# Attention block, one core: the last head group's PV in two sessions, with the row maxima's product behind it

## The chip, the cores and the metric

The kernel runs on one core of a Trainium2 chip. The metric is device time in microseconds (us) of one execution; lower is better. Every number is float32 in memory; the large products run as float32 or as float32 split in a high and a low part.

## What is computed

```python
def reference(x, w_qkv, b_qkv, w_proj, b_proj, pos_independent, ffn_kernel, input_scale, kernel_scale, ffn_bias):
    # x: 16 x 512 x 256; 16 heads of 16
    xn = _layernorm(x, axis=-1)
    qkv = xn @ w_qkv.T + b_qkv
    q, k, v = ...                                   # reshape to heads
    att = einsum('bhqd,bhkd->bhqk', q, k) / sqrt(16)
    att = att + bias                                # per head, from positions alone
    att = softmax(where(causal, att, -inf))
    attn = einsum('bhqk,bhkd->bhqd', att, v) @ w_proj.T + b_proj
    ffn = quantise_e4m3(xn.bf16) @ quantise_e4m3(ffn_kernel) + ffn_bias
    return x + attn + ffn
```

## The kernel before, in words

A **body** `b` handles one of the 16 batches and overlaps it with its neighbours. Bodies 0, 14 and 15 are written out; bodies 1 to 13 are a loop on every engine. A body has four **units** `g` of four heads each, and a unit has twelve **slots** `k`. I write a place as (unit, slot), so (0, 3) is slot 3 of the body's first unit.

In every slot TensorE (PE) makes two interleaved streams. `scores_T` (L640, L643) makes transposed scores of this unit into one of three banks `scoreT_a/b/c`; ScalarE (ACT) turns each into `probs` with an exponential (L925), GpSimd (POOL) masks the diagonal (L1201), and `pv` (L666) multiplies the masked probabilities of the *previous* unit with V and a column of ones. `scores` (L617) makes plain scores two units ahead into `score_a/b/c`, from which VectorE (DVE) takes row maxima (L1003). A slot's `scores_T` waits for the exponential of three slots earlier, its `scores` for the row maximum of three slots earlier. All waits are in order on an engine: what stands behind a waiting instruction waits too.

Other work hangs behind slots by tables of (unit, slot): `PV_AT` (PV of the previous unit; for unit 3 of body b-1 that is in body b), `MT_AT` (the product that transposes the maxima, L601), `QK_AT`, `V_AT`, `FF_AT` (the quantised product, L593), `PJ_AT`, `T_AT` (transpose of x two bodies ahead, L558). All of these write two banks in turn, `misc_a` and `misc_b`, and each waits until the former user of its bank was read. A PV stands whole in one place, except that of unit 0, which `PV_REST_AT` cuts: key tile 0 at (1, 0), tiles 1 to 3 at (1, 3).

The stations around the change:

- **Maxima to scores.** ACT `max_hi` (L840) in slot 2, PE `job_MT` (L601), ACT `max_T` (L844), then SP `load_max` issues four 4 KB transfers (L341). Slot 0 of the next unit waits for all four.
- **PV to the denominators.** ACT `out_T` (L898) copies PV's bank; then `send_attn` issues two transfers, `attn` (L354) and `denominators` (L355). For units 0 to 2 SP issues them (`regroup`); for unit 3 ACT itself does, right behind `out_T`, after a wait for that copy. DVE `invert` (L1010) takes reciprocals at (0, 6); SP stores them (`store_recips`, L396) and loads them spread over the rows of `xn` (`spread_recips`, L408); POOL divides (L1235) in unit 1.
- **x two bodies ahead.** PE transposes at (3, 9) into `misc_a` and `misc_b`; ACT copies each twice (`XH_evac` L821, `XB_evac` L824); DVE makes the low halves (`T_lo`, L985), of `misc_a` at (3, 10) and of `misc_b` at (0, 0). DVE's statistics of x stand in unit 1 (L973, L981).
- **FF.** Its second half writes `misc_b` at (2, 0), which QK's last low part (DVE L991, at (1, 10)) must have read.

## Time and profile before

| what | us |
|---|---|
| median of 3 runs | 810.89 |
| lowest, highest | 809.94, 812.63 |
| the profiled execution, whole time | 810.14 |
| its span in the profile | 808.4 |
| PE busy, of the span | 752.4 (93%) |
| DVE, ACT, POOL busy | 624.6, 578.6, 531.1 |

The span is the time between the first and last instruction of the profiled execution; 1.7 us of that execution lie outside it. A view of the profile is a timeline (instructions of one engine in order of time, in brackets the idle time before it and who ended it), a table of waits (who waited for whom, summed), or busy time by stretch. The loop repeats every 46.3 us; the rows below are from the body that starts at about 421.9 us, unless said otherwise.

### The profile page before, as it was taken

Reading aid. Unit: us, or ns where it says so; the run is one execution under the profiler, and the core shown is the slowest. Engines: PE = TensorE matmul, PEld = TensorE weight load, DVE = VectorE, ACT = ScalarE, POOL = GpSimd, SP = SyncE. Lnnn points to the kernel's source line nnn. Section 1 sums busy time; section 2 is a strip of 40 time slices with the busy share of each in tenths; the row PEclk is TensorE's granted clock in tenths of the full one; section 3 lists DMA queues with packets and bytes.
Section 4 is the critical chain, followed back from the end, with each engine's and each line's share of the span. In section 5 each row is a group of like instructions: output and inputs, shape, how many; then the busy total and the mean of one; then the engine's idle time right before and its main releaser. Section 6 shows DMA issues by size and latency. Waiting matters only on the chain.

```text
span 808.4 us, 23158 instructions
## 1 busy us (share of the span) xinstructions
PE 752.4 (93%) x6313; PEld 515.3 (64%) x6313; DVE 624.6 (77%) x2395; ACT 578.6 (72%) x1258; POOL 531.1 (66%) x525
## 2 busy tenths in 40 slices
PE   6889999999999999999999999999999999999883
PEld 3556566676666766666676667667676666667552
DVE  3869878887978888787887888798788878888612
ACT  3347868777877868777886777777787777777570
POOL 6435568676666767577666857666676767757570
PEclk8859999999999999999999999999999999999997
DMA  5603333534333253333434243443335334343202
GB/s 172 235 2 140 120 123 114 172 115 151 138 145 136 106 189 119 129 137 145 166 117 149 112 159 112 164 140 145 121 119 179 131 122 138 146 146 114 78 18 86
DMA packets 55612, 106.07 MB, mean 131 GB/s; under 512 B 10528, under 2 KB 30496, under 8 KB 55584
## 3 DMA queue, kind: packets, MB, share of 16 engines
q1 hardware_dynamic: 52680, 102.96, 36.2%
q10 hardware_dynamic: 2904, 2.77, 1.1%
q8 instruction: 13, 0.21, 0.1%
q14 instruction: 15, 0.12, 0.1%
HBM read 18.68 MB, written 8.91 MB: 34 GB/s over the span
## 4 chain that ended last, share of the span: by engine, by line
PE 69%; ACT 7%; DVE 7%; issue 6%; DMA 6%; SPq 3%; ACTq 1%; DVEq 1%; POOL 0%; POOLq 0%
PE misc_a L666 13%; PE misc_a L550 10%; PE misc_b L550 10%; PE scoreT_b L640 8%; PE scoreT_a L640 5%; PE score_a L617 4%; PE score_c L617 4%; DMA x_ring<-in_L_attn_x 4%; PE misc_b L666 3%; SPq L341 3%; ACT probs L925 3%; PE misc_b L601 2%; ACT xnT_hi L821 2%; PE scoreT_c L640 2%; DVE row_max L1003 1%
## 5 line engine op out<-in xcount | busy, mean ns | idle before, releaser
L1201 POOL TENSOR_SCALAR_AFFINE_SELECT probs<-probs 128x512 f32<-128x512 f32 x256 | 161.7, 642 | 231.1 <-ACT probs L925 229.5
L1003 DVE CUSTOM_DVE_ANT_0 score_b<-score_b,causal_mask_q 128x384 f32<-128x384 f32 (+3 forms) x321 | 162.0, 522 | 95.8 <-PE score_b L617 95.6
L1003 DVE CUSTOM_DVE_ANT_0 score_a<-score_a,causal_mask_q 128x512 f32<-128x512 f32 x319 | 174.9, 565 | 6.5 <-PE score_a L617 3.2
L925 ACT ACTIVATE probs<-scoreT_b 128x384 f32<-128x384 f32 (+1 forms) x256 | 134.4, 525 | 63.5 <-PE scoreT_b L640 21.1
L1003 DVE CUSTOM_DVE_ANT_0 score_c<-score_c,causal_mask_q 128x256 f32<-128x256 f32 (+3 forms) x384 | 172.0, 476 | 3.0 <-PE score_c L617 2.8
L925 ACT ACTIVATE probs<-scoreT_a 128x512 f32<-128x512 f32 (+1 forms) x256 | 145.4, 568 | 4.5 <-PE scoreT_a L643 3.7
L1003 DVE DVE_READ_ACCUMULATOR2_ANT row_max<- 128x1 f32 x1024 | 145.6, 142 | 0.0
L925 ACT ACTIVATE probs<-scoreT_c 128x384 f32<-128x384 f32 (+1 forms) x256 | 135.9, 531 | 3.4 <-PE scoreT_c L643 3.0
L666 PE MATMUL misc_a<-probs,v_ones 128*32 128x128 f32 (+3 forms) x1536 | 132.1, 440 | 0.4 <-POOL probs L1201 0.4
L640 PE MATMUL scoreT_b<-stacks 64*128 64x384 f32 (+3 forms) x320 | 120.0, 394 | 5.7 <-ACT probs L925 5.7
L617 PE MATMUL score_b<-stacks 64*128 64x384 f32 (+3 forms) x321 | 118.4, 401 | 1.4 <-DVE row_max L1003 1.4
L640 PE MATMUL scoreT_c<-stacks 64*128 64x256 f32 (+3 forms) x384 | 106.6, 309 | 8.9 <-ACT probs L925 8.9
L617 PE MATMUL score_a<-stacks 64*128 64x512 f32 x319 | 111.1, 380 | 2.7 <-DVE row_max L1003 2.6
L640 PE MATMUL scoreT_a<-stacks 64*128 64x512 f32 (+3 forms) x320 | 108.1, 358 | 5.0 <-DMA low_features<-neg_max_T 2.4
L640 PEld LDWEIGHTS scoreT_b<-stacks 64*128 64x128 f32 x320 | 57.0, 185 | 72.6 <-ACT probs L925 39.9
L617 PE MATMUL score_c<-stacks 64*128 64x256 f32 (+3 forms) x384 | 99.6, 313 | 0.5 <-DVE row_max L1003 0.2
L640 PEld LDWEIGHTS scoreT_c<-stacks 64*128 64x128 f32 x384 | 68.9, 187 | 15.9 <-ACT probs L925 14.0
L666 PEld LDWEIGHTS misc_a<-probs,v_ones 128*32 128x32 f32 x1536 | 59.7, 109 | 28.6 <-issue 12.3
L617 PEld LDWEIGHTS score_c<-stacks 64*128 64x128 f32 x384 | 65.8, 189 | 5.5 <-DVE row_max L1003 5.0
L617 PEld LDWEIGHTS score_a<-stacks 64*128 64x128 f32 x319 | 55.4, 188 | 20.4 <-DVE row_max L1003 16.9
L640 PEld LDWEIGHTS scoreT_a<-stacks 64*128 64x128 f32 x320 | 57.4, 187 | 12.0 <-issue 6.8
L898 ACT ACTIVATE out_T<-misc_a 128x512 f32<-128x512 f32 x48 | 28.7, 599 | 42.4 <-PE misc_a L666 42.4
(241 smaller groups left out, 1957.3 us busy)
## 6 DMA issues: line engine op xcount, KB each, us to landing
stacks<-qk_parts SPq DMA_DIRECT2D x128, 512.0 KB, 3.9
x_ring<-in_L_attn_x SPq DMA_DIRECT2D x16, 512.0 KB, 3.3
xn<-recips SPq DMA_DIRECT2D x31, 256.0 KB
out<-x_ring SPq DMA_DIRECT2D x15, 512.0 KB, 3.0
attn<-out_T SPq DMA_DIRECT2D x48, 128.0 KB, 2.6
stacks<-neg_max_T SPq DMA_DIRECT2D x128, 4.0 KB
attn<-out_T ACTq DMA_DIRECT2D x16, 128.0 KB, 2.7
low_features<-neg_max_T SPq DMA_DIRECT2D x124, 4.0 KB
```

Of the source, the lines that this page charges most:

```text
L341: eng.dma_start(max_rows(g, h), MTS[2 * TT * h:2 * TT * h + 2 * TT, g % 2, :].bitcast(F32)) \
L550: last = mm(o, l(ct), r(ct), start=(ct == 0 and i == 0), stop=(ct == CT - 1 and i == 2))
L601: last = mm(bank[0:HU * 2 * TT, 0:P], MX[:, g % 2, 32 * part:32 * part + 32], ident[:, :], start=(part == 0), stop=(part == 1))
L617: last = mm(SB_[n % 3][:, o:o + w], STK[rows, u, 0, P * qt:P * qt + P], STK[rows, u, 1, 0:w], start=True, stop=True)
L640: last = mm(bank, STK[rows, u, 1, P * j:P * j + P], STK[rows, u, 0, P * j:T], start=True, stop=(g >= 2))
L666: last = mm(bank[32 * i:32 * i + 32, P * j:T], VA[:, j, HU * g + i, :, :].rearrange("p d a -> p (d a)"), probs(g, j)[:, i, :], start=(j == ...
L821: A(XH[:, ct, :], misc_of("T", ct)[:, :], ACT.Copy).then_inc(xh_ready, 1)
L898: A(OT[:, :], misc_of("PV", g)[:, :], ACT.Copy).then_inc(ot_ready, 1)
L925: A(probs_slot(g, k), STB[(SLOTS * g + k) % 3][:, 0:w], ACT.Exp).then_inc(exp_done, 1)
L1003: last = V.tensor_tensor_reduce(bank, bank, CMQ[:, T - w:T], 1.0, LEAST, ALU.add, ALU.max, MX[:, g % 2, 8 * h + 4 + qt:8 * h + 5 + qt])
L1201: last = GP.affine_select(out=d, in_=d, compare_op=ALU.is_ge, fill=0.0, base=0, pattern=[[0, HU], [1, P]], channel_multiplier=-1)
```

## The change

1. PV of unit 3 is cut as that of unit 0 is: key tile 0 at (0, 0) of the next body, tiles 1 to 3 at (0, 3). The maxima's product that stood between its tile 0 and tile 1 now stands behind tile 3.
2. In the first unit ACT runs `out_T` ahead of `max_T`, and no longer issues the two transfers of unit 3, but for the last body. SP issues them, ahead of its four loads of the maxima.
3. SP spreads the reciprocals behind the load of the next body's first stack, not ahead of it.
4. On DVE: the low halves of x at (3, 9) and (0, 2), the reciprocals at (0, 8), statistics of x at (1, 3), (1, 3), (1, 6), (1, 6) and their sum at (1, 7), the quantiser's steps one slot later.

```diff
-PV_AT = [(1, 0), (2, 3), (3, 3), (0, 3)]
-PV_REST_AT = {0: (1, 3)}
+PV_AT = [(1, 0), (2, 3), (3, 3), (0, 0)]
+PV_REST_AT = {0: (1, 3), 3: (0, 3)}
...
-XL_AT, FIRST_XL_AT = [(3, 10), (0, 0)], [(0, 3), (0, 3)]
-INVERT_AT, LAST_INVERT_AT = (0, 6), (3, 8)
-STATS_AT, AGGR_AT = [(1, 2), (1, 3), (1, 5), (1, 8)], (1, 9)
-MAGIC_AT = [(2, 0), (2, 1), (2, 2)]
+XL_AT, FIRST_XL_AT = [(3, 9), (0, 2)], [(0, 3), (0, 3)]
+INVERT_AT, LAST_INVERT_AT = (0, 8), (3, 8)
+STATS_AT, AGGR_AT = [(1, 3), (1, 3), (1, 6), (1, 6)], (1, 7)
+MAGIC_AT = [(2, 1), (2, 2), (2, 3)]
...
                 load_stack(b, 3)
+                if not first:
+                    regroup(b - 1, 3, False)
                 load_max(b, 1)
...
                 if not first:
                     store_recips(b - 1)
-                    spread_recips(b - 1, last)
 
                 if not last:
                     wait_alone(sp, (w_loaded, 16), (st_ready, ROW * b + SLOTS),
                                (ql_ready, 4 * (b + 1) + 2))
                     load_stack(b + 1, 0)
+                if not first:
+                    spread_recips(b - 1, last)
                 load_max(b, 2)
...
-                elif then:
+                elif then and g < 3:
                     job_MT(*then)
...
                 if TT - 1 in tiles:
                     last.then_inc(pv_done, 1)
+                if 0 not in tiles and then and g == 3:
+                    job_MT(*then)
...
-                if g == 3:
-                    act.wait_ge(ot_ready, 4 * b + 4)
+                if g == 3 and isinstance(b, int) and b == B - 1:
+                    act.wait_ge(ot_ready, 4 * B)
                     send_attn(act, b, 3)
...
                         if k == OUT_AT and not (first and g == 0):
+                            if g == 0:
+                                out_T(pb, pg, False)
                             if not (last and g == 3):
                                 max_T(*((b, g + 1) if g < 3 else (b + 1, 0)))
-                            out_T(pb, pg, first and pg == 0)
+                            if g > 0:
+                                out_T(pb, pg, first and pg == 0)
```

**PE, start of the first unit of a loop body.** Before, around (0, 3): the last transposed scores of slot 3 (L643), PV's key tile 0 (512 columns), the maxima's product (L601), tile 1.

```order
L643 MATMUL scoreT_a<-low_features 128x512
L541 ISA
L664 ISA [waits xnT_lo_written]
L666 MATMUL misc_a<-probs,v_ones 32x512 [waits probs_masked]
L666 MATMUL misc_a<-probs,v_ones 32x512 x3
L598 ISA
L541 REGISTER_ALU [waits max_hi_written]
L601 MATMUL misc_b<-ident_f,row_max 32x128 [waits xnT_lo_written]
L601 MATMUL misc_b<-neg_ident_f,row_max 32x128
L664 REGISTER_ALU
L666 MATMUL misc_a<-probs,v_ones 32x384 [waits probs_masked]
```

Now, behind slot (0, 0), whose last row is the first here:

```order
L646 MATMUL scoreT_a<-low_features 128x512
L544 ISA
L667 ISA [waits xnT_lo_written]
L669 MATMUL misc_a<-probs,v_ones 32x512 [waits probs_masked]
L669 MATMUL misc_a<-probs,v_ones 32x512 x3
L637 REGISTER_ALU
L643 MATMUL scoreT_b<-stacks 128x512 [waits exp_done]
```

and the end of the second session, at (0, 3):

```order
L669 MATMUL misc_a<-probs,v_ones 32x128 [waits probs_masked]
L669 MATMUL misc_a<-probs,v_ones 32x128 x3
L601 ISA
L544 REGISTER_ALU [waits max_hi_written]
L604 MATMUL misc_b<-ident_f,row_max 32x128 [waits xnT_lo_written]
L604 MATMUL misc_b<-neg_ident_f,row_max 32x128
L637 REGISTER_ALU
L643 MATMUL scoreT_b<-stacks 128x384 [waits exp_done]
```

Tile 0 went three slots forward, in front of the scores of slots 1 to 3, and waits there for the low half that leaves `misc_a` free; the maxima's product went behind tile 3.

**ACT, from slot (0, 3) to slot (0, 4).** Before:

```order
L925 ACTIVATE probs<-scoreT_a 128x512 [waits scoresT_in_psum]
L843 ISA
L844 ACTIVATE neg_max_T<-misc_b 32x128 [waits max_T_in_psum]
L892 ISA
L896 ISA [waits pv_done]
L898 ACTIVATE out_T<-misc_a 128x512 [waits denominators0_regrouped,out_T0_regrouped]
L354 ISA [waits out_T_written]
L354 DMA attn<-out_T 64x512
L355 DMA denominators<-out_T 32x1x64
L920 REGISTER_ALU
L925 ACTIVATE probs<-scoreT_b 128x384 [waits scoresT_in_psum]
```

Now:

```order
L933 ACTIVATE probs<-scoreT_a 128x512 [waits scoresT_in_psum]
L897 ISA
L901 ISA [waits pv_done]
L903 ACTIVATE out_T<-misc_a 128x512 [waits denominators0_regrouped,out_T0_regrouped]
L848 ISA
L849 ACTIVATE neg_max_T<-misc_b 32x128 [waits max_T_in_psum]
L928 REGISTER_ALU
L933 ACTIVATE probs<-scoreT_b 128x384 [waits scoresT_in_psum]
```

The two issues and the wait ahead of them left ACT; the two copies changed places.

**SP, first unit.** Before:

```order
L341 DMA low_features<-neg_max_T 2x4x128 [waits max_T_written]
L341 DMA low_features<-neg_max_T 2x4x128 x3
L479 REGISTER_ALU
L480 ISA [waits out_stored]
L371 ISA [waits x_loaded]
L371 DMA x_ring<-in_L_attn_x 128x4x256
```

Now:

```order
L390 ISA
L354 ISA [waits out_T_written]
L354 DMA attn<-out_T 64x512
L355 DMA denominators<-out_T 32x1x64
L381 ISA
L341 DMA low_features<-neg_max_T 2x4x128 [waits max_T_written]
L341 DMA low_features<-neg_max_T 2x4x128 x3
L481 REGISTER_ALU
L482 ISA [waits out_stored]
L371 ISA [waits x_loaded]
L371 DMA x_ring<-in_L_attn_x 128x4x256
```

The two transfers of unit 3 stand ahead of the four loads and wait for `out_T`.

**DVE, unit 1, ahead of the low part of QK that FF's second half waits for.** Before, at slots 8 and 9:

```order
L973 BN_STATS bn_six<-x_ring 128x6
L347 REGISTER_ALU
L1003 ISA score_a,row_max<-score_a,causal_mask_q 128x256 [waits scores_in_psum,x_loaded]
L1003 ISA row_max 128x1
L1003 ISA score_a,row_max<-score_a,causal_mask_q 128x128
L1003 ISA row_max 128x1
L347 ISA [waits neg_mean_done,var_eps_done]
L981 BN_AGGR mean_var<-bn_six 128x2 [waits bn_stats_done,x_loaded]
```

Now, at slots 6 and 7:

```order
L981 BN_STATS bn_six<-x_ring 128x6
L981 ISA
L981 BN_STATS bn_six<-x_ring 128x6
L347 REGISTER_ALU
L1011 ISA score_b,row_max<-score_b,causal_mask_q 128x384 [waits scores_in_psum,x_loaded]
L1011 ISA row_max 128x1
L998 REGISTER_ALU
L999 SCALAR_TENSOR_TENSOR qk_parts<-misc_a,b_qkv,qk_parts 128x512 [waits qk_hi_written]
L347 ISA [waits neg_mean_done,var_eps_done]
L989 BN_AGGR mean_var<-bn_six 128x2 [waits bn_stats_done,x_loaded]
```

The statistics and their sum moved from slots 8 and 9 to slots 6 and 7.

## Rows read from the trace of the kernel before

**Rows 1.** The page, DMA issues: count, KB each, median us from issue to landing.

```profile
stacks<-qk_parts SPq DMA_DIRECT2D x128, 512.0 KB, 3.9
```

**Rows 2.** Busy time of one loop body: stretch, length, PE, PEld, DVE, ACT, POOL, clock.

```profile
421.30:467.60 46.30, 44.75 (x396) 31.00 (x395) 38.24 (x150) 35.74 (x79) 32.60 (x31) 1.00 0.39 139
```

**Rows 3.** Waits of the whole span: us in total, times, longest.

```profile
PE scoreT_c L640 <- ACT probs L925: 8.9, 15, 0.6
PE misc_b L593 <- DVE qk_parts L991: 6.3, 15, 0.4
```

**Rows 4.** Timeline of PE, first unit: start, duration, line, shape, count [idle before].

```profile
422.29 0.39 PE L643 MATMUL scoreT_a<-low_features 64*128 64x512 f32 x1
422.51 0.39 PE L640 MATMUL scoreT_b<-stacks 64*128 64x512 f32 x1
...
423.77 0.49 PE L640 MATMUL scoreT_c<-stacks 64*128 64x512 f32 x1 [0.63 <-ACT probs L925]
...
424.60 0.39 PE L643 MATMUL scoreT_a<-low_features 64*128 64x512 f32 x1
424.93 1.06 PE L666 MATMUL misc_a<-probs,v_ones 128*32 128x512 f32 x8
...
427.63 0.44 PE L640 MATMUL scoreT_b<-stacks 64*128 64x384 f32 x1
...
430.52 0.44 PE L640 MATMUL scoreT_b<-stacks 64*128 64x384 f32 x1 [0.15 <-ACT probs L925]
```

**Rows 5.** Timeline of ACT and its DMA issues (ACTq), first unit.

```profile
427.94 0.60 ACT L898 ACTIVATE out_T<-misc_a 128x512 f32<-128x512 f32 x1 [1.22 <-PE misc_a L666]
428.70 0.57 ACTq L354 DMA_DIRECT2D attn<-out_T  x1
429.30 0.56 ACTq L355 DMA_DIRECT2D denominators<-out_T  x1
429.98 0.49 ACT L925 ACTIVATE probs<-scoreT_b 128x384 f32<-128x384 f32 x1 [1.45 <-issue]
```

**Rows 6.** Timeline of DVE, first unit.

```profile
422.45 0.69 DVE L985 TENSOR_TENSOR xnT_lo<-misc_a,xnT_hi 128x512 fp32r<-128x512 f32 x1
...
431.60 0.55 DVE L1010 RECIPROCAL denominators_inv<-denominators 128x64 f32<-128x64 f32 x1 [1.72 <-DMA denominators<-out_T]
```

**Rows 7.** Timeline of SP's DMA issues, unit 3 and first unit.

```profile
419.73 0.62 SPq L355 DMA_DIRECT2D denominators<-out_T  x1
...
426.74 2.72 SPq L341 DMA_DIRECT2D low_features<-neg_max_T  x4
```

**Rows 8.** Timeline of PE, unit 1, where PV already has two sessions.

```profile
434.25 0.44 PE L640 MATMUL scoreT_a<-stacks 64*128 64x512 f32 x1
...
434.61 0.50 PE L643 MATMUL scoreT_a<-low_features 64*128 64x512 f32 x1
435.04 1.07 PE L666 MATMUL misc_a<-probs,v_ones 128*32 128x512 f32 x8
436.03 0.50 PE L640 MATMUL scoreT_b<-stacks 64*128 64x512 f32 x1
...
437.65 0.40 PE L601 MATMUL misc_b<-ident_f,row_max 128*32 128x128 f32 x2
...
439.49 0.44 PE L640 MATMUL scoreT_b<-stacks 64*128 64x384 f32 x1
```

**Rows 9.** Timeline of PE: FF's second half at (2, 0).

```profile
447.26 0.61 PE L593 MATMUL misc_b<-ffn_w_q,xq 128*128 128x256 bf16 x4 [0.44 <-DVE qk_parts L991]
```

**Rows 10.** Timeline of DVE, end of unit 1.

```profile
444.68 0.42 DVE L973 BATCH_NORM_STATS2 bn_six<-x_ring 128x6 f32 x1
...
445.59 0.37 DVE L981 BATCH_NORM_AGGREGATE mean_var<-bn_six 128x2 f32<-128x6 f32 x4
...
446.46 0.75 DVE L991 SCALAR_TENSOR_TENSOR qk_parts<-misc_b,b_qkv,qk_parts 128x512 fp32r<-128x512 f32 x1
```

**Rows 11.** Timeline of ACT, end of unit 1.

```profile
445.05 1.12 ACT L832 ACTIVATE qk_parts<-misc_b,b_qkv 128x1024 fp32r<-128x1024 f32 x1 [0.53 <-PE misc_b L550]
```

## The prediction, made before the changed kernel ran

> **What bounds the kernel now.** I read the busy time by stretch first. One loop body takes 46.30 us, PE is busy for 44.75 of them, DVE for 38.24, ACT for 35.74, POOL for 32.60, with a granted clock of 1.00, which is the 2.4 GHz level [rows 2]. The span of 808.4 us is about sixteen such bodies with a start and an end that the change leaves alone. So PE's own row of instructions is the path, and the change adds and removes no product: it can only win back PE's pauses, 1.55 us of a body, or add to them.
>
> The waits of the whole span name the pauses: `scoreT_c` waits 15 times for an exponential, 8.9 us in all, and FF's second half 15 times for DVE, 6.3 us [rows 3]. The timeline places the first at (0, 2): two transposed scores start 1.26 us apart, at 422.51 and 423.77, with 0.63 us idle, while ACT still copies x two bodies ahead [rows 4]. From 422.29 to 424.60 PE does three slots; without the slow one that leaves 2.31 - 1.26 = 1.05 for two, 0.52 each, so the slow step contains 1.26 - 0.52 = 0.74 us of pause. A smaller one, 0.15 us idle, stands at 430.52 [rows 4]: there PE waits for the exponential of slot (0, 4), which ACT starts only at 429.98, behind `out_T` at 427.94 and two DMA issues [rows 5]. The third is 0.44 us ahead of FF's second half [rows 9]. These three are what the change aims at.
>
> **PV's tile 0 goes into the pause at (0, 2).** The eight matmul records of tile 0 begin at 424.93 now; they would begin behind the score that starts at 422.29 [rows 4]. Unit 1 shows what such a session costs: from its last score row to tile 0 0.43 us, from tile 0 to the next score 435.04 to 436.03 = 0.99 us; the second session with its maxima's product 437.65 to 439.49 = 1.84 us; 2.83 together [rows 8]. The single session of unit 3 takes 424.93 to 427.63 = 2.70 us, and 0.33 us to get into it from the score at 424.60; an ordinary step between two scores is 422.29 to 422.51 = 0.22 us [rows 4]. Two sessions are 2.83 plus two entries less one ordinary step: 2.83 + 0.86 - 0.22 = 3.47 with the dearer entry, 2.83 + 0.66 - 0.22 = 3.27 with the cheaper. Against 2.70 + 0.33 = 3.03 the cut costs 0.24 to 0.44 us; I take the middle, 0.34.
>
> The Trainium skill (TensorEngine Tiling (Array Packing), Key Properties) speaks against the cut: changing the tiling mode drains TensorE, and the cut adds one change into 32-column tiles and one out. The 0.34 us above are what this case's rows charge for that pair, so the rule is right in its sign and too small here to undo the gain.
>
> Tile 0 must also wait for `misc_a`, until DVE made x's first low half. That ran from 422.45 for 0.69 us, to 423.14 [rows 6], and the session could start at 422.29 + 0.43 = 422.72. If DVE were no earlier, PE would wait 0.42 us. The product moves one slot up on DVE, ahead of one pair of row maxima, so it should end near 422.8: I take 0.1, bounds 0 and 0.42. Sum of this part: 0.74 - 0.34 - 0.10 = **0.30 us** of a body (bounds -0.12 and 0.50). The same DVE row then comes ahead of row maxima that PE needs three slots later; PE is by then 0.5 us later in slots 1 to 3 too, so I charge nothing. The second low half, at (0, 2), must be there for the maxima's product at the end of the second session, some 1.8 us later: hidden by PV's tiles 1 to 3.
>
> **ACT loses two issues.** From `out_T` at 427.94 to the next exponential at 429.98 ACT spends 2.04 us, of which 0.57 + 0.56 are issues and the rest mostly waits around them [rows 5]. Without them that exponential comes when its scores are there, near 428.0, and the pause at 430.52 goes: 0.15 us by its row, a little more by the distance of the starts; I take **0.20** (0.15 to 0.30).
>
> The Trainium skill (DMA: Bandwidth & Descriptors, Issuing engines are not separate DMA queues) says that issuing from several engines saves only the sequencer's time, usually small beside the transfer. By that the move would be worth nothing and the sum below 0.20 us a body less. The ACT rows speak against it: the sequencer's time is 1.2 us in the row of exponentials that PE waits for.
>
> DVE no longer stands 1.72 us for the denominators [rows 6]: their transfer is issued about 1 us earlier and the reciprocal comes two slots later. Where that helps PE no row shows by itself; between 0 and 0.2 (the size of the pause above) I take **0.10**.
>
> **FF's second half.** DVE's low part of QK starts at 446.46 and ends as PE starts [rows 9, 10]. Its input, ACT's copy, ends at 445.05 + 1.12 = 446.17 [rows 11]. The statistics (0.42 us) and their sum (0.37), which stood in the two slots ahead of it [rows 10], move to where DVE waits for PE anyway. So DVE can start at 446.17: **0.29 us**, bounds 0 and the 0.44 that the row shows.
>
> **What it may cost: the maxima of unit 1.** SP issued the four loads from 426.74 to 429.46 [rows 7], and slot (1, 0), which starts at 434.25 [rows 8], waits for them. Now they stand behind `out_T` and two issues. `out_T` starts at 427.94 - 0.30 = 427.64 at the latest (PE is 0.30 earlier), the first issue follows 0.76 later as it did on ACT [rows 5], 428.40, the two take 0.60 and 0.62 [rows 5, 7], the loads start at 429.62 and the last of them 2.1 later, at 431.7. A small transfer lands 2.3 us after its issue: the denominators, 429.30 to 431.60 [rows 5, 6]. That is 434.0. At the earliest it is 0.6 less, since the maxima's product no longer stands inside PV and SP may issue sooner than ACT did: 433.4. PE, 0.5 us earlier, wants them at 433.75. So a new pause of 0 to 0.3 us; I take **0.10**. Behind the loads on SP stand the load of x (used in the second unit) and the store of the reciprocals, which comes later by the two slots; the spread behind the stack's load is awaited by POOL's division in unit 1, with microseconds to spare: nothing charged. The quantiser's steps one slot later cost nothing either, since POOL reads them in the next body.
>
> **Sum.** 0.30 + 0.20 + 0.10 + 0.29 - 0.10 = 0.79 us of a body. The pauses at (0, 2) and at FF occur in 14 of the 16 bodies at full size (the last body follows one that moves no x, the first has no PV there; the statistics end with body 13). 14 x 0.79 = 11.1 us: the span goes from 808.4 to 797.3 us, the execution from 810.14 to 799.0. The median of the runs shown is 0.75 above the profiled execution; 810.89 - 11.1 = **799.8 us**.
>
> **Rivals.**
>
> *A new pause eats most of it.* Tile 0 waits the full 0.42 us for DVE and the cut costs 0.44, which leaves 0.74 - 0.86 = -0.12 in the first part; the maxima take their 0.3. Then 0.20 + 0.29 - 0.12 - 0.3 + 0 = 0.07 us a body, 1.0 us: 809.9. Half of that misfortune: 0.43 us, 6.0 us, 804.9. For it: three of the new distances are a few tenths. Against: DVE's row stands behind one pair of maxima only.
>
> *Slower: the maxima come late.* The four loads stand behind a 128 KB transfer and ahead of the 512 KB of x on the same queue. If they take not 2.3 but 3.9 us, as the stacks' transfers do [rows 1], they land at 435.0 to 435.6 where PE wants them at 433.75: a pause of 1.3 to 1.9 us against a gain of 0.89, so 0.4 to 1.0 us lost in each of 15 bodies, and 817 to 826 us. It decides from a landing 3.2 us behind the issue on. Against: before, two other transfers were issued beside them too, and nobody waited.
>
> *PE's pauses chain.* If PE's earlier scores let DVE and ACT keep ahead in the rest of the body as well, the pauses that the 1.55 us hold beside the three go too: 1.15 us a body, 16 us, 794.8.
>
> *The move from ACT to SP does nothing* (the skill's rule above as a mechanism: ACT's exponentials catch up anyway before PE needs them). Then 0.20 and 0.10 are missing: 0.49 us, 6.9 us, 804.0.
>
> **How the numbers follow.** Forecast, 796 to 803: 0.57. More, below 796: 0.10. Move without effect or half of the misfortune, 803 to 808.4: 0.14. Within 0.3% (2.4 us, about what a measurement of this kernel can tell from no change), 808.5 to 813.3: 0.10. Slower: 0.09. Faster is therefore 0.57 + 0.10 + 0.14 = 0.81. For eight in ten the range leaves out the slower case and the ends: 794.5 to 807.
>
> **What would show it.** In the changed profile: the step at (0, 2) without a pause of 0.6 us and PV's first eight records between slots 0 and 1; the exponential of (0, 4) right behind the maxima's copy and no pause at (0, 7); FF's second half with 0.1 to 0.2 us idle; DVE's reciprocal without a wait; and a body of 45.5 us. It is wrong if PE shows a pause at (1, 0) for `low_features<-neg_max_T`, or one ahead of tile 0 for `xnT_lo`, of more than 0.4 us.

## The result

| | before | changed |
|---|---|---|
| median, us | 811.53 | 791.89 |
| lowest to highest | 809.94 to 812.63 | 790.76 to 793.01 |
| ratio, 95% interval | | 0.9759 (0.9733 to 0.9786) |
| span of the profiled execution | 808.4 | 789.0 |

The kernel before ran once more beside the changed one, so its median is 811.53 us of four executions here. The change saves 19.6 us, or 2.4%. The forecast was 799.8 us with a range down to 794.5: the direction was right, the gain was 1.8 times the 11.1 us that I had summed, and 791.9 lies below the range.

The busy times by stretch of the changed kernel, one loop body of 45.1 us, answer to [rows 2] (same columns). PE is busy 44.29 of 45.10 us, so 0.8 us of the 1.55 us of pauses are left. The other 0.46 us of the gain came out of PE's *busy* time (44.75 before), although its products are the same ones: what the profile calls busy (the ends of products in it are modelled) held waiting too. DVE's and ACT's busy times are within 0.6 us of what they were.

```profile
413.50:458.60 45.10, 44.29 (x392) 30.17 (x392) 38.84 (x149) 35.83 (x80) 32.34 (x31) 1.00 0.39 142
```

The timeline of PE at the start of the first unit answers to [rows 4]:

```profile
413.06 0.42 PE L646 MATMUL scoreT_a<-low_features 64*128 64x512 f32 x1
413.60 1.07 PE L669 MATMUL misc_a<-probs,v_ones 128*32 128x512 f32 x8
414.59 0.49 PE L643 MATMUL scoreT_b<-stacks 64*128 64x512 f32 x1
...
414.93 0.39 PE L643 MATMUL scoreT_c<-stacks 64*128 64x512 f32 x1
...
415.40 0.40 PE L643 MATMUL scoreT_a<-stacks 64*128 64x512 f32 x1
...
415.95 1.50 PE L669 MATMUL misc_a<-probs,v_ones 128*32 128x384 f32 x24
417.29 0.41 PE L604 MATMUL misc_b<-ident_f,row_max 128*32 128x128 f32 x2
...
417.84 0.44 PE L643 MATMUL scoreT_b<-stacks 64*128 64x384 f32 x1
...
420.51 0.44 PE L643 MATMUL scoreT_b<-stacks 64*128 64x384 f32 x1
```

Tile 0 stands between slots 0 and 1, and neither slot 2 (414.93) nor slot 7 (420.51) has idle time in brackets any more. ACT in the same place answers to [rows 5]: from `out_T` to the exponential of slot 4 it is 0.82 us, where it was 2.04.

```profile
417.67 0.60 ACT L903 ACTIVATE out_T<-misc_a 128x512 f32<-128x512 f32 x1 [0.62 <-PE misc_a L669]
418.16 0.25 ACT L849 ACTIVATE neg_max_T<-misc_b 32x128 fp32r<-32x128 f32 x1
418.49 0.49 ACT L933 ACTIVATE probs<-scoreT_b 128x384 f32<-128x384 f32 x1
```

SP's issues answer to [rows 7], and PE's start of the second unit to the first of [rows 8]:

```profile
418.45 0.53 SPq L354 DMA_DIRECT2D attn<-out_T  x1
419.02 0.62 SPq L355 DMA_DIRECT2D denominators<-out_T  x1
419.87 2.73 SPq L341 DMA_DIRECT2D low_features<-neg_max_T  x4
423.08 0.41 SPq L371 DMA_DIRECT2D x_ring<-in_L_attn_x  x1
423.78 0.35 SPq L396 DMA_DIRECT2D recips<-denominators_inv  x1
425.66 1.25 SPq L377 DMA_DIRECT2D stacks<-qk_parts  x2
427.10 2.01 SPq L408 DMA_DIRECT2D xn<-recips  x2
```

```profile
424.04 0.44 PE L643 MATMUL scoreT_a<-stacks 64*128 64x512 f32 x1
```

The loads of the maxima end their issue at 422.60 and slot (1, 0) starts at 424.04 without a wait. FF's second half waits 0.20 us where it waited 0.44 [rows 9]:

```profile
436.85 0.61 PE L596 MATMUL misc_b<-ffn_w_q,xq 128*128 128x256 bf16 x4 [0.20 <-DVE qk_parts L999]
```

**Where the 19.4 us of the span come from.** I set the start of each slot's last transposed score in one trace against the other. A loop body takes 46.32 us before and 45.13 now (mean of ten bodies, from slot (0, 0) of body 2 to that of body 12, in each trace): 1.19 us. In the body of the rows the gain is 0.56 us from slot (0, 0) to (0, 4), 0.42 from there to (1, 0), 0.21 at FF, and nothing after that. Bodies 1 to 14 together give 16.8 us. Body 0 gives 0.7 and body 15 gives 2.4, where I had put nothing; some 0.5 is lost outside the bodies.

Half of body 15's 2.4 us is TensorE's clock. Its second unit ran at a granted clock of 0.86 before and 1.00 now (busy time by stretch, before and changed):

```profile
757.75:767.43 9.68, 9.51 (x83) 5.48 (x84) 6.81 (x31) 6.30 (x15) 3.14 (x5) 0.86 0.19 69
738.82:747.25 8.43, 8.24 (x83) 5.18 (x82) 6.32 (x27) 5.90 (x14) 2.02 (x4) 1.00 0.23 80
```

That is 1.25 us for the same products. A granted clock of 1.00 is the 2.4 GHz level, 0.50 the 1.2 GHz level, and 0.86 a stretch with some of each: read in steps of 1 us, the kernel before has 1.00 up to 757 us, 0.50 from 758 to 760, and 1.00 again from 761 on. Ahead of that it has two pauses of PE, 1.52 and 1.14 us, the changed one a single one of 1.42 us (shown below).

### The profile page after: what moved, and what is told of

Its sections match the earlier page's. It is cut to its first block, busy times and chain, and to the rows that moved or that the text cites. A ratio compares the mean times of both kernels' runs of the same rounds, so it can differ in the third digit from the quotient of the medians.

```text
span 789.0 us, 23171 instructions
## 1 busy us (share of the span) xinstructions
PE 743.6 (94%) x6313; PEld 503.1 (64%) x6313; DVE 633.0 (80%) x2395; ACT 580.0 (74%) x1258; POOL 531.3 (67%) x525
## 4 chain that ended last, share of the span: by engine, by line
PE 74%; DVE 9%; ACT 7%; issue 5%; DMA 2%; DVEq 1%; SPq 1%; POOL 1%; ACTq 0%; POOLq 0%
PE misc_a L669 14%; PE misc_a L553 13%; PE misc_b L553 10%; PE scoreT_b L643 9%; PE scoreT_a L643 5%; PE score_c L620 4%; PE score_a L620 3%; PE misc_b L669 3%; PE misc_b L604 3%; PE scoreT_b L646 2%; ACT qk_parts L837 2%; DVE row_max L1011 2%; PE scoreT_a L646 1%; ACT probs L933 1%; DVE qk_parts L999 1%
## 5 line engine op out<-in xcount | busy, mean ns | idle before, releaser
L933 ACT ACTIVATE probs<-scoreT_b 128x384 f32<-128x384 f32 (+1 forms) x256 | 132.4, 517 | 43.9 <-PE scoreT_b L646 20.1
L933 ACT ACTIVATE probs<-scoreT_a 128x512 f32<-128x512 f32 (+1 forms) x256 | 143.2, 559 | 6.2 <-PE scoreT_a L646 5.1
L933 ACT ACTIVATE probs<-scoreT_c 128x384 f32<-128x384 f32 (+1 forms) x256 | 133.7, 522 | 3.2 <-PE scoreT_c L646 2.7
L669 PE MATMUL misc_a<-probs,v_ones 128*32 128x128 f32 (+3 forms) x1536 | 128.6, 438 | 2.8 <-DVE xnT_lo L993 1.2
L643 PE MATMUL scoreT_b<-stacks 64*128 64x384 f32 (+3 forms) x320 | 121.2, 398 | 1.8 <-ACT probs L933 1.7
L643 PE MATMUL scoreT_a<-stacks 64*128 64x512 f32 (+3 forms) x320 | 105.9, 350 | 6.6 <-DMA low_features<-neg_max_T 3.8
L620 PE MATMUL score_a<-stacks 64*128 64x512 f32 x319 | 109.0, 373 | 2.4 <-DVE row_max L1011 2.4
L643 PEld LDWEIGHTS scoreT_b<-stacks 64*128 64x128 f32 x320 | 56.9, 185 | 78.7 <-ACT probs L933 45.8
L643 PE MATMUL scoreT_c<-stacks 64*128 64x256 f32 (+3 forms) x384 | 103.1, 301 | 0.3 <-ACT probs L933 0.3
L620 PE MATMUL score_c<-stacks 64*128 64x256 f32 (+3 forms) x384 | 96.4, 305 | 0.5 <-DVE row_max L1011 0.2
L669 PEld LDWEIGHTS misc_a<-probs,v_ones 128*32 128x32 f32 x1536 | 53.5, 109 | 40.2 <-issue 20.0
L643 PEld LDWEIGHTS scoreT_c<-stacks 64*128 64x128 f32 x384 | 69.0, 187 | 1.5 <-ACT probs L933 0.8
L643 PEld LDWEIGHTS scoreT_a<-stacks 64*128 64x128 f32 x320 | 57.5, 187 | 11.7 <-issue 6.6
L837 ACT ACTIVATE qk_parts<-misc_a,b_qkv 128x1024 fp32r<-128x1024 f32 x32 | 35.7, 1116 | 30.8 <-PE misc_a L553 30.8
```

What stands on the lines that cost most here:

```text
L620: last = mm(SB_[n % 3][:, o:o + w], STK[rows, u, 0, P * qt:P * qt + P], STK[rows, u, 1, 0:w], start=True, stop=True)
L643: last = mm(bank, STK[rows, u, 1, P * j:P * j + P], STK[rows, u, 0, P * j:T], start=True, stop=(g >= 2))
L669: last = mm(bank[32 * i:32 * i + 32, P * j:T], VA[:, j, HU * g + i, :, :].rearrange("p d a -> p (d a)"), probs(g, j)[:, i, :], start=(j == ...
L837: A(qk_part(m, 0), misc_of("QK", m)[:, :].unsqueeze(1).broadcast_to([P, 2, T]), ACT.Identity, bias=BQ[:, bias:bias + 1]).then_inc(qh_ready, 1)
L933: A(probs_slot(g, k), STB[(SLOTS * g + k) % 3][:, 0:w], ACT.Exp).then_inc(exp_done, 1)
```

## The experiments

The start and the end of a run differ by a us or two between executions of the same start (slot (0, 0) of body 0 lies at 43.2 to 45.3 us in these profiles). The body's period is steadier, so I give it for each run beside the median, taken as above from the one profiled execution. Each ratio is to executions of the kernel before that were taken beside that run.

In most profiles the ten bodies agree within 0.1 us, at a granted clock of 1.00. In four they don't, as some bodies ran at 0.96 or 0.97: one in e1 (47.62 us, the nine others 46.55), two in e8 (47.8, the others 45.76), four in s2 (48.7, the others 47.07) and five in s5 (48.4, the others 46.58). For these four the period is a mixture, and the loss at full clock is the smaller number. The profiled execution of s5 (828.48 us) is also the slowest of its five (816.24 to 828.48), so its period is not comparable with its median.

| kernel | body, us | median, us | ratio to before, 95% interval |
|---|---|---|---|
| before | 46.32 | 811.53 | |
| changed | 45.13 | 791.89 | 0.9759 (0.9733 to 0.9786) |
| *changed, one part undone* | | | |
| e1: PV of unit 3 whole | 46.66 | 816.22 | 1.0034 (1.0013 to 1.0056) |
| e1b: the same, low halves as before | 45.82 | 804.14 | 0.9902 (0.9871 to 0.9933) |
| e2: ACT issues | 45.32 | 794.91 | 0.9784 (0.9751 to 0.9817) |
| e3: statistics | 45.32 | 793.29 | 0.9772 (0.9740 to 0.9805) |
| e4: both low halves | 45.50 | 798.32 | 0.9815 (0.9788 to 0.9842) |
| e5: reciprocals at (0, 6) | 45.02 | 790.06 | 0.9743 (0.9703 to 0.9784) |
| e6: maxima's product first | 46.55 | 813.82 | 1.0031 (1.0013 to 1.0048) |
| e8: spread ahead of the stack | 46.16 | 809.44 | 0.9980 (0.9952 to 1.0009) |
| e10: second low half at (0, 0) | 45.07 | 791.76 | 0.9766 (0.9736 to 0.9795) |
| e9: e10 and maxima's product first | 45.47 | 798.05 | 0.9842 (0.9814 to 0.9869) |
| e7: PV of unit 0 whole too | 45.91 | 804.58 | 0.9920 (0.9897 to 0.9944) |
| *before, one part done* | | | |
| s1: cut only | 46.39 | 812.93 | 1.0015 (0.9991 to 1.0038) |
| s4: cut, first low half early | 45.97 | 805.43 | 0.9920 (0.9895 to 0.9946) |
| s2: SP issues | 47.72 | 828.11 | 1.0208 (1.0153 to 1.0263) |
| s5: maxima's product behind, out_T first | 47.49 | 818.52 | 1.0085 (1.0051 to 1.0119) |
| *attempts to go further* | | | |
| v1: e5, FF's second half a slot later | 45.02 | 791.98 | 0.9757 (0.9734 to 0.9780) |
| v2: e5 and e10 | 45.02 | 791.98 | 0.9763 (0.9734 to 0.9792) |
| v3: v2, quantiser's steps as before | 45.12 | 793.13 | 0.9770 (0.9742 to 0.9798) |

**The cut, undone.**

```diff
-PV_AT = [(1, 0), (2, 3), (3, 3), (0, 0)]
-PV_REST_AT = {0: (1, 3), 3: (0, 3)}
+PV_AT = [(1, 0), (2, 3), (3, 3), (0, 3)]
+PV_REST_AT = {0: (1, 3)}
```

> The changed kernel with PV of unit 3 whole again at (0, 3), the maxima's product behind its tile 0; all else as changed. Theory A (the cut fills the pause at (0, 2), and slots 1 to 3 also run faster since their exponentials and maxima are ready): the body goes from 45.13 to about 45.7 us, that is 0.55 us a body or some 8 us in all (797 us). Theory B (the sizes on record: the cut brings 0.30 us a body): 45.45, some 4 us (796 us is out of its reach; it says 796 or less, near 795.6 at most). A rival C (the cut brings nothing, ACT's lighter row does it all): no change, 45.15.

It lost 1.53 us a body (1.42 without the one body of lower clock), and the run ended slower than the kernel before. That is not the cut's worth. Without the cut the maxima's product stands behind tile 0 again, and x's second low half, which it waits for, was left at (0, 2). PE's timeline shows the pause: the product starts 1.41 us behind tile 0 (427.35), where it is 0.88 us in e1b.

```profile
428.76 0.41 PE L604 MATMUL misc_b<-ident_f,row_max 128*32 128x128 f32 x2 [0.34 <-DVE xnT_lo L993]
```

So the edit undid one of two edits that need each other. e1b puts both low halves back as well.

```diff
 (as above, and)
-XL_AT, FIRST_XL_AT = [(3, 9), (0, 2)], [(0, 3), (0, 3)]
+XL_AT, FIRST_XL_AT = [(3, 10), (0, 0)], [(0, 3), (0, 3)]
```

> The changed kernel with PV of unit 3 whole at (0, 3) and x's low halves at (3, 10) and (0, 0) as before; SP's, ACT's and the other DVE edits stay. Theory A (the cut fills the pause at (0, 2), the exponentials and maxima being ready then): against the run with the low halves at (3, 10) and (0, 0) and the cut (body 45.52) it loses about 0.3 us more, body 45.8. Theory B (ACT's and SP's edits alone bring most of the gain): 45.4 or less. Theory C (without the cut the other edits bring nothing or cost): 46.3 or more, no faster than the kernel before.

45.82, as theory A had it. Against e4 (cut kept, low halves back, 45.50) it loses 0.32 us; against the changed kernel 0.69. But this is not the cut alone: with PV whole the maxima's product stands inside it again, and its place alone is worth 0.40 us (e9, below). With the low halves late and the product ahead of tiles 1 to 3, s1 finds no gain from the cut.

**The low halves, undone.**

```diff
-XL_AT, FIRST_XL_AT = [(3, 9), (0, 2)], [(0, 3), (0, 3)]
+XL_AT, FIRST_XL_AT = [(3, 10), (0, 0)], [(0, 3), (0, 3)]
```

> The changed kernel with x's low halves at (3, 10) and (0, 0) again. If the earlier slot matters: PV's tile 0 waits some 0.3 to 0.6 us for xnT_lo at (0, 0), body 45.4 to 45.7, 4 to 8 us. If it doesn't: 45.15 and no more than 0.5 us in all.

0.38 us a body, all of it between slots 0 and 1, where tile 0 waits for `misc_a`. This is the bound of 0.42 us of the prediction, with the rows that it was made from. e10 moves the second half alone:

```diff
-XL_AT, FIRST_XL_AT = [(3, 9), (0, 2)], [(0, 3), (0, 3)]
+XL_AT, FIRST_XL_AT = [(3, 9), (0, 0)], [(0, 3), (0, 3)]
```

> The changed kernel with x's second low half at (0, 0) again (the first stays at (3, 9)). DVE then makes it ahead of the maxima of slot 1. If (0, 2) was needed to keep those maxima ahead of PE: 0.1 to 0.3 us a body lost. If it was free: 45.1 within 0.05.

45.07: its move to (0, 2) gives nothing, all of e4's loss is the first half's.

**The cut alone, on the kernel before.**

```diff
-PV_AT = [(1, 0), (2, 3), (3, 3), (0, 3)]
-PV_REST_AT = {0: (1, 3)}
+PV_AT = [(1, 0), (2, 3), (3, 3), (0, 0)]
+PV_REST_AT = {0: (1, 3), 3: (0, 3)}
```

> The kernel before with the cut alone: PV's tile 0 at (0, 0), tiles 1 to 3 at (0, 3) with the maxima's product ahead of them; ACT still issues, low halves and all else as before. Theory A: most of the cut's gain is there at once; with 0.4 us of wait for xnT_lo, body 45.9 to 46.1 (4 to 6 us faster). Theory C (the cut pays only once ACT's issues and the wait for the denominators are gone): 46.3 or more, no faster.

No gain. The timeline of PE shows why: one pause took the place of the other, and a small one stands at the head of the second session.

```profile
425.12 1.06 PE L666 MATMUL misc_a<-probs,v_ones 128*32 128x512 f32 x8 [0.60 <-DVE xnT_lo L985]
...
427.73 0.40 PE L601 MATMUL misc_b<-ident_f,row_max 128*32 128x128 f32 x2 [0.18 <-ACT row_max L840]
```

s4 adds the early first half:

```diff
 (as above, and)
-XL_AT, FIRST_XL_AT = [(3, 10), (0, 0)], [(0, 3), (0, 3)]
+XL_AT, FIRST_XL_AT = [(3, 9), (0, 0)], [(0, 3), (0, 3)]
```

> The kernel before with the cut and x's first low half at (3, 9) (the second stays at (0, 0)); ACT issues, the maxima's product ahead of tiles 1 to 3. If the cut alone brought nothing only because tile 0 waited 0.4 us for xnT_lo: body 46.37 to 45.95, 5 us faster than before. If ACT's row (out_T and two issues, 2 us) holds PE at slots 7 and 8 anyway: 46.1 to 46.3.

45.97, that is 0.35 us a body below the kernel before. It is the arrangement for which the prediction's first sum, 0.30 us, was in fact made: its durations came from unit 1, where the maxima's product stands at the head of the second session. The timeline of PE, from slot 1 to the product:

```profile
420.77 0.50 PE L640 MATMUL scoreT_b<-stacks 64*128 64x512 f32 x1
...
421.81 0.39 PE L643 MATMUL scoreT_a<-low_features 64*128 64x512 f32 x1
422.38 0.40 PE L601 MATMUL misc_b<-ident_f,row_max 128*32 128x128 f32 x2 [0.18 <-ACT row_max L840]
```

Slots 1 to 3 take 1.04 us from first to last row, as in the changed kernel (415.63 - 414.59); then 0.57 us pass to the second session, 0.18 of them idle, as its first product waits for ACT.

**The place of the maxima's product.**

```diff
-                elif then and g < 3:
+                elif then:
                     job_MT(*then)
...
-                if 0 not in tiles and then and g == 3:
-                    job_MT(*then)
```

> The changed kernel with the maxima's product ahead of PV's tiles 1 to 3 at (0, 3), as unit 0 has it. It comes 1.3 us earlier there; ACT reads it only behind out_T, so nobody is served earlier, and it waits for x's second low half, made at (0, 2). If that wait bites: 0.3 us or more a body. If the place is free either way: 45.1 within 0.05.

1.42 us a body, and the wait table blames the low half (14 times, 17.9 us in all). The timeline of PE:

```profile
428.84 0.41 PE L604 MATMUL misc_b<-ident_f,row_max 128*32 128x128 f32 x2 [1.27 <-DVE xnT_lo L991]
```

DVE makes that half behind the maxima of slot 2, and PE gets there 1.3 us earlier. So the product's place and (0, 2) belong together as well. e9 takes that wait away by e10's edit and then moves the product:

```diff
 (as above, and)
-XL_AT, FIRST_XL_AT = [(3, 9), (0, 2)], [(0, 3), (0, 3)]
+XL_AT, FIRST_XL_AT = [(3, 9), (0, 0)], [(0, 3), (0, 3)]
```

> The changed kernel with the maxima's product ahead of PV's tiles 1 to 3, and x's second low half at (0, 0), so that nothing waits for it. If the place of the product matters by itself (PV's last tile, and with it out_T on ACT, comes 0.4 us later against slot 4, and the product at the head of a session waits): 0.2 to 0.5 us a body more than with the low half moved alone. If only the wait for xnT_lo made the earlier run slow: the same as that one, within 0.05.

45.47 against e10's 45.07: the place of the product behind PV is worth 0.40 us a body by itself. 0.25 of it is there by slot 4, 0.15 comes at the start of unit 1.

**ACT's issues.**

```diff
-                if not first:
-                    regroup(b - 1, 3, False)
                 load_max(b, 1)
...
-                if g == 3 and isinstance(b, int) and b == B - 1:
-                    act.wait_ge(ot_ready, 4 * B)
+                if g == 3:
+                    act.wait_ge(ot_ready, 4 * b + 4)
                     send_attn(act, b, 3)
```

> The changed kernel with unit 3's two transfers issued by ACT again, behind out_T and ahead of the copy of the maxima and of slot 4's exponential. Theory A (ACT's 2 us hold up three slots, not one): the body goes from 45.13 to 45.5 to 45.6, 6 us in all, and the last body, which has no QK product to hide them, loses 1.5 us more: 798 to 800. Theory B (0.20 us a body on record): 45.33, 2.8 us, 795. By the skill's rule that the issuing engine matters little: no change.

0.19 us a body, the size of theory B, but at another place: only 0.05 is lost by slot 8, where the exponentials of slots 4 to 6 are awaited; 0.15 is at (1, 0). There ACT's copy of the maxima, now behind the two issues, is the likely cause. Body 15 loses nothing, against theory A. The timeline of ACT in this run:

```profile
420.41 0.60 ACT L901 ACTIVATE out_T<-misc_a 128x512 f32<-128x512 f32 x1 [0.61 <-PE misc_a L667]
421.17 0.57 ACTq L354 DMA_DIRECT2D attn<-out_T  x1
421.77 0.56 ACTq L355 DMA_DIRECT2D denominators<-out_T  x1
422.45 0.27 ACT L847 ACTIVATE neg_max_T<-misc_b 32x128 fp32r<-32x128 f32 x1 [1.44 <-issue]
422.62 0.47 ACT L931 ACTIVATE probs<-scoreT_b 128x384 f32<-128x384 f32 x1
```

The issues cost ACT what they did, but `out_T` itself starts earlier against PE's slot 4, as the product no longer stands inside PV; the exponential is then just in time.

s2 does the same edit the other way, on the kernel before (SP issues, ahead of the loads of the maxima; ACT not):

```diff
+                if not first:
+                    regroup(b - 1, 3, False)
                 load_max(b, 1)
...
-                if g == 3:
-                    act.wait_ge(ot_ready, 4 * b + 4)
+                if g == 3 and isinstance(b, int) and b == B - 1:
+                    act.wait_ge(ot_ready, 4 * B)
```

> The kernel before with one edit: SP issues unit 3's two transfers, ahead of its loads of the maxima; PV whole, all tables as before. Theory A (ACT's two issues hold up the exponentials of slots 4 to 6): body 46.34 to 45.9, 6 us. Theory B (0.20 us on record): 46.1. The rival on record (the maxima come late, as SP waits for out_T before their loads): a pause at (1, 0), 46.3 or more, and low_features<-neg_max_T as its cause.

17 us *slower*, 1.4 us a body. In the body of the rows PE is 0.42 us ahead by slot (0, 8), as theory A said, has lost that again by (0, 11), and stands 1.6 us behind at (2, 0). The bodies at full clock lose 0.75 us; the rest of the 1.4 is the clock, granted at 0.86 in unit 2 of four of the ten bodies, each time behind such a pause. The rival on record was right that the maxima come late; it named the wrong unit. The timelines of PE and of SP:

```profile
457.28 0.49 PE L642 MATMUL scoreT_a<-stacks 64*128 64x512 f32 x1 [1.49 <-DMA stacks<-neg_max_T]
```

```profile
443.31 0.41 SPq L371 DMA_DIRECT2D x_ring<-in_L_attn_x  x1
443.92 0.35 SPq L396 DMA_DIRECT2D recips<-denominators_inv  x1
447.04 1.36 SPq L408 DMA_DIRECT2D xn<-recips  x2
448.63 1.22 SPq L377 DMA_DIRECT2D stacks<-qk_parts  x2
449.98 3.72 SPq L341 DMA_DIRECT2D stacks<-neg_max_T  x4
```

Between the store of the reciprocals and their spread lie 3.1 us, 1.5 before (432.23 to 433.75 in the trace of the kernel before): the store is now issued 0.6 us behind the 512 KB of x, not 2.2 us. Stack and maxima stand behind that wait. The changed kernel has the slow store too (3.0 us from issue to landing in it, 1.5 before); only the wait is elsewhere.

**The spread's place on SP.** The changed kernel with the spread ahead of the stack's load, as before:

```diff
                     store_recips(b - 1)
+                    spread_recips(b - 1, last)
...
                     load_stack(b + 1, 0)
-                if not first:
-                    spread_recips(b - 1, last)
```

> The changed kernel with the spread of the reciprocals ahead of the next body's first stack load on SP again, as before. The run with only SP's two transfers moved lost 1.6 us a body at (2, 0), waiting for the maxima of unit 2. If the place of the spread is what that loss hangs on (SP stands for the stored reciprocals, and stack and maxima behind it come late): this kernel loses 1 to 1.6 us a body, 45.1 to 46.2 or more, 805 us and up, with a pause at (2, 0) for stacks<-neg_max_T. If the loss came from elsewhere (the reciprocals' own delay at (0, 6)): 45.15, 792.

1.04 us a body, 809.44 us: without this edit the change gains nothing that the runs can tell from zero. Again (2, 0) waits for the maxima of unit 2; the timelines of PE and SP:

```profile
445.40 0.50 PE L642 MATMUL scoreT_a<-stacks 64*128 64x512 f32 x1 [1.35 <-DMA stacks<-neg_max_T]
```

```profile
432.20 0.35 SPq L396 DMA_DIRECT2D recips<-denominators_inv  x1
435.20 1.35 SPq L408 DMA_DIRECT2D xn<-recips  x2
436.79 1.22 SPq L377 DMA_DIRECT2D stacks<-qk_parts  x2
438.13 3.62 SPq L341 DMA_DIRECT2D stacks<-neg_max_T  x4
```

In the changed kernel the stack goes out at 425.66 and the spread only then; the wait for the stored reciprocals hides behind the stack's wait and issue (the store lands 3.0 us after 423.78, the stack's issue ends at 426.91).

The pause at (2, 0) is 0.3 to 2.1 us long in e8, 1.1 us on the mean. Behind its four longest ones unit 2 ran at a lower clock. Busy time by stretch of unit 2 in two neighbouring bodies:

```profile
445.40:457.61 12.21, 12.05 (x100) 8.50 (x102) 8.70 (x31) 8.60 (x19) 7.81 (x10) 0.86 0.25 99
492.35:503.21 10.86, 10.71 (x100) 7.70 (x102) 9.12 (x32) 8.94 (x20) 8.59 (x11) 1.00 0.29 111
```

In steps of 1 us the first of the two is at 0.50 from 447 to 449 and at 1.00 again from 450 on. So 0.64 us of e8's 1.04 are the late maxima, the rest the clock that fell behind them.

**The product behind a whole PV**, on the kernel before, with `out_T` ahead of the copy of the maxima; ACT issues:

```diff
-                    if j == 0 and then:
+                    if j == 0 and then and g < 3:
                         job_MT(*then)
...
+                if then and g == 3:
+                    job_MT(*then)
...
+                            if g == 0:
+                                out_T(pb, pg, False)
...
-                            out_T(pb, pg, first and pg == 0)
+                            if g > 0:
+                                out_T(pb, pg, first and pg == 0)
```

> The kernel before with PV of unit 3 whole at (0, 3), the maxima's product behind its last tile and out_T ahead of the copy of the maxima; ACT still issues. If an earlier out_T takes away the pause at slots 7 and 8: up to 0.4 us a body gained there (46.34 to 45.9), unless ACT's issues now delay the maxima so that (1, 0) waits for their loads. If the pause hangs on the issues themselves: 46.3.

In the body of the rows it gains 0.30 us by slot 8 and 0.46 us by (1, 1): an earlier `out_T` does remove most of the pause at slots 7 and 8 with ACT still issuing. Then (2, 0) waits for the maxima of unit 2 (13 times, up to 3.0 us) and the run ends slower than before. The rows of SP are those of s2: the maxima's loads go out later, x behind them, and the store 0.6 us behind x (446.26 and 446.88; the spread follows at 449.98).

**Reciprocals and statistics.**

```diff
-INVERT_AT, LAST_INVERT_AT = (0, 8), (3, 8)
+INVERT_AT, LAST_INVERT_AT = (0, 6), (3, 8)
```

> The changed kernel with the reciprocals at (0, 6) again. Their transfer lands about 1.5 us after DVE gets there. If DVE's wait holds PE: 0.1 to 0.3 us a body, 45.2 to 45.4. If it doesn't: 45.15 (DVE waits 1 us or so and no engine waits for it).

DVE waits again for the denominators, and the body is 0.11 us *shorter*. In the loop its wait held nobody:

```profile
420.48 0.56 DVE L1018 RECIPROCAL denominators_inv<-denominators 128x64 f32<-128x64 f32 x1 [1.23 <-DMA denominators<-out_T]
```

In body 15 it did hold PE. There DVE waits 1.54 us for the denominators, and PE then 2.00 us for a row maximum that the changed kernel doesn't wait for:

```profile
736.47 0.45 PE L620 MATMUL score_b<-stacks 64*128 64x256 f32 x1 [2.00 <-DVE row_max L1011]
```

Unit 0 of that body takes 11.21 us against 10.39, and unit 1, at a granted clock of 0.90, takes 9.31 against 8.43. So e5 gains 1.5 us in fourteen bodies and loses 1.7 us in the last.

```diff
-STATS_AT, AGGR_AT = [(1, 3), (1, 3), (1, 6), (1, 6)], (1, 7)
+STATS_AT, AGGR_AT = [(1, 2), (1, 3), (1, 5), (1, 8)], (1, 9)
```

> The changed kernel with the statistics of x and their sum at the slots they had before. All theories: FF's second half waits 0.2 us more in bodies 0 to 13, body 45.13 to 45.34, 3 us in all, 794.9. If instead nothing moves, the 0.21 us came from elsewhere.

0.20 us a body at FF's second half and nowhere else.

**The price of a cut.** Unit 0's PV whole at (1, 3) in the changed kernel:

```diff
-PV_AT = [(1, 0), (2, 3), (3, 3), (0, 0)]
-PV_REST_AT = {0: (1, 3), 3: (0, 3)}
+PV_AT = [(1, 3), (2, 3), (3, 3), (0, 0)]
+PV_REST_AT = {3: (0, 3)}
```

> The changed kernel with unit 0's PV whole at (1, 3), where it was cut before and after. There it fills no pause that a row shows, so this gives the price of a cut alone. On record: 0.24 to 0.44 us a cut, so the body gets faster, 45.13 to 44.8, 4 us. If ACT or DVE then run dry during the long session and PE waits behind it: no gain or a loss.

0.79 us a body *lost*. (The maxima's product moves too, from the head of the second session to behind tile 0.) Where the cut kernel shows no pause, one appears: slots 1 to 3 of unit 1 are the 512-column ones, and without tile 0 ahead of them PE runs into DVE. The timeline of PE in this run, then the same three slots in the changed kernel:

```profile
430.92 0.49 PE L643 MATMUL scoreT_b<-stacks 64*128 64x512 f32 x1
...
432.25 0.50 PE L620 MATMUL score_c<-stacks 64*128 64x512 f32 x1 [0.45 <-DVE row_max L1011]
...
432.90 0.50 PE L646 MATMUL scoreT_a<-low_features 64*128 64x512 f32 x1
```

```profile
425.82 0.50 PE L643 MATMUL scoreT_b<-stacks 64*128 64x512 f32 x1
...
426.93 0.49 PE L646 MATMUL scoreT_a<-low_features 64*128 64x512 f32 x1
```

From the first row of slot 1 to the last of slot 3 PE takes 432.90 - 430.92 = 1.98 us without the cut and 426.93 - 425.82 = 1.11 us with it.

**Going further.** v1 has e5's edit and FF's second half one slot later:

```diff
-FF_AT = [(2, 0), (2, 0)]
+FF_AT = [(2, 0), (2, 1)]
```

> The changed kernel with the reciprocals at (0, 6) and FF's second half behind slot (2, 1) rather than (2, 0). The reciprocals at (0, 6) gave 0.1 us a body, FF's half no longer waits 0.25 us for DVE: body 45.13 to 44.75, 5 to 6 us, 786 to 787 us. If ACT's copy of FF then holds up the exponentials: 45.0, 790.

45.02, just what e5 alone gives: the 0.2 us pause is gone, and PE is no further by slot (2, 4). v2 has e5's and e10's edits, v3 the quantiser's steps back too:

```diff
-MAGIC_AT = [(2, 1), (2, 2), (2, 3)]
+MAGIC_AT = [(2, 0), (2, 1), (2, 2)]
```

> The changed kernel with the reciprocals at (0, 6) and x's second low half at (0, 0). If the two small gains add: body 45.13 to 44.95, some 2.5 us, 789 us. If both sit on the same pause: 45.0.

> The same with the quantiser's steps at (2, 0), (2, 1), (2, 2) again. On record it costs nothing: the same body as the other within 0.05. If DVE's 2 us of it hold up the maxima right behind unit 2's start: 0.1 to 0.4 us a body more.

45.02: the two small gains are one. v3 has 0.10 us a body more on the mean, but half of its bodies are as short as v2's, so the quantiser's later slots are worth 0.10 us at most. No version beats the changed kernel by more than the runs can tell; e5's 790.06 us comes nearest. v1, v2 and v3 all have e5's reciprocals, and in their profiles body 15 shows e5's pause of 2.0 us and takes 42.4 to 44.0 us, where the changed kernel takes 38.75.

## Why the prediction was too small, by its own steps

**The sum, term by term.** On record a body gains 0.30 (cut and early low half) + 0.20 (ACT) + 0.10 (DVE) + 0.29 (FF) - 0.10 (maxima) = 0.79 us. Measured it is 0.56 + 0.42 for ACT's stretch as a whole + 0.21 + 0 = 1.19 us. The cut's term and ACT's were too small, and 3.1 us in bodies 0 and 15 were not in the sum at all. The ceiling that I read from [rows 2], 1.55 us of pauses beside 44.75 us of work, was no ceiling, as the busy time fell as well.

**Right.** PE is the path, the three pauses named are where the loop's gain comes from, and they are gone or halved. The wait of tile 0 for `xnT_lo`: 0.10 us on record, and 413.60 - 413.06 = 0.54 us into the session, against 0.43 in unit 1 [rows 8], is 0.11. Its bound of 0.42 us is e4's 0.38. FF's term, 0.29 us, measured 0.21 (0.20 by e3).

**Right by luck.** The sum for the cut with the early low half, 0.30 us, is 0.35 in s4, the arrangement it was made for. Two errors cancel in it: slots 1 to 3 take 1.04 us there and not 1.35, and the way into the second session 0.57 us and not 0.33. Putting the product behind PV took away the second error alone.

**The step that failed first: slots 1 to 3 were mis-sized (the cut's term, 0.30 against 0.56).** From the score of slot 0 to slot 4 the record's sum is 0.43 + 0.10 + 0.99 for tile 0, 1.68 for slots 1 to 3 (422.51 to 424.93, less the pause of 0.74), and 1.84 for the rest: 5.04 us. Measured: 413.06 to 414.59 = 1.53, then 414.59 to 415.95 = 1.36, then 415.95 to 417.84 = 1.89. The first and the third are right within 0.05; the middle is 0.32 too long. I had taken the "ordinary" step of 0.52 us from steps that were not free: the two slots beside the pause were slow as well. That they waited in parts too short for the views, which show no idle time under 0.15 us, is an inference. e7 shows the same from the other side: take a session out from ahead of such slots and PE waits there. So the "price of a cut" of 0.24 to 0.44 us was a sum over rows that did not hold the other half of the account. The Trainium skill (TensorEngine Tiling (Array Packing), Key Properties) says that changing the tiling mode drains TensorE. No run measured that drain by itself; whatever it costs is outweighed here in both units.

**ACT's pause was mis-sized (0.20 against 0.42), and its cause was only half seen.** The row that I read says 0.15 us idle at slot 7; s2 recovers 0.42 us by slot 8, as slot 8 was late too. And not the issues alone cause it: with the cut and the product behind PV, giving them back to ACT costs 0.05 us at these slots (e2), while with PV whole, `out_T` first and the product behind PV gain 0.30 us by slot 8 with ACT still issuing (s5). The two edits win back the same pause. The maxima's product was a step whose move I priced only as an earlier start of SP's issues; it is worth 0.40 us (e9 against e10). The Trainium skill (DMA: Bandwidth & Descriptors, Issuing engines are not separate DMA queues) calls the sequencer's time usually small beside the transfer; the 0.19 us a body of e2 is small, though not nothing.

**DVE's freed time, 0.10 us on record, is nothing in the loop.** e5 brings its wait back and is 0.11 us a body faster. It is worth having in body 15, where e5 loses 0.8 us in unit 0 and 0.9 us by the clock behind it.

**The maxima of unit 1, -0.10 on record, cost nothing in the loop.** They do in body 15, whose PE has no QK product to fill its slots; there I had put no change at all. The timeline of PE in body 15, the kernel before first, then the changed one:

```profile
753.52 0.44 PE L640 MATMUL scoreT_b<-stacks 64*128 64x384 f32 x1 [1.52 <-ACT probs L925]
...
756.25 0.38 PE L617 MATMUL score_b<-stacks 64*128 64x256 f32 x1 [1.14 <-DVE row_max L1003]
```

```profile
738.48 0.49 PE L643 MATMUL scoreT_a<-stacks 64*128 64x512 f32 x1 [1.42 <-DMA low_features<-neg_max_T]
```

The two pauses for ACT and DVE, 2.66 us together, go; one of 1.42 us for the maxima at (1, 0) is new. Unit 0 comes out 1.46 us shorter (11.85 to 10.39), unit 1 1.25 us by the clock, and unit 2 0.35 us longer: 2.4 us in all. That the two pauses made the clock fall in the kernel before is argued from their order (it fell within 2 us of the second) and not tested; behind the changed kernel's one pause of 1.42 us it stayed at 1.00.

**The spread's move, charged with nothing, carries the rest.** I looked only at who awaits the spread, and not at what stands behind it on SP. e8: 1.04 us a body, 0.64 of it at full clock. The rival "slower: the maxima come late" described this failure, at unit 1 and for 817 to 826 us; s2 made it real at unit 2, with 828.11 us. What kept it from the changed kernel was the edit that I had dismissed in half a sentence.

**A rival had the size.** "PE's pauses chain" gave 1.15 us a body and 794.8 us; the loop gained 1.19. Its mechanism isn't what happened: no gain appears in units 1 and 3, or in unit 2 behind FF. What was won beside the bracketed idle time lies at the three pauses themselves.

**Open.** PE loses 0.4 us at (0, 11) in s2, where its score waits for a row maximum. The reciprocals are not later there (441.55 is 9.30 us into the body, 431.60 is 9.31 in the kernel before): DVE stands as long as before for the denominators, and PE's lead seems to run into that. Nothing was run to test it, nor what makes the clock fall behind one pause and not another. The 0.7 us of body 0 are 0.23 at FF and 0.5 at (2, 7), the second not explained.

## What to carry to other kernels

The idle time in brackets understated two of the three pauses here, as the slots beside them were slow as well, so take the "free" step from a place where nothing is short, or count the stretch as a whole against the sum of its work. When an in-order queue gets work earlier or in another order, price every instruction behind the moved one, not only who reads the moved one's result. Parts of a reordering are not additive: here three of four parts, done alone, gained nothing or cost up to 17 us, and undoing a single one cost up to 22 us; test the pairs that share a buffer or a queue together. And look at the granted clock of every stretch before a loss is put down to a wait alone.
